# Tower: the inverse norm of the output as one power on POOL and a spreading copy on DVE

## The chip, the cores and the metric

The kernel runs as one program on one core of a Trainium2 chip. The metric is the device time of one execution in microseconds. The five engines work from queues of their own, in order: PE (TensorE), DVE (VectorE), ACT (ScalarE), POOL (GpSimd) and SP (SyncE), which here only issues DMAs.

## The reference, cut to what matters

A small language model: a token tower of two layers, then one layer of linear attention and a gated MLP. All is fp32. The step that the change touches is in the tower's attention:

```python
def _scan_attn(x, ...):                      # x: (32, 256, 128), 8 heads of 16
    ...
    attn = cum_gZ / (cum_g + EPS)
    o = jnp.einsum('bhsd,bhsde->bhse', q, attn)
    nrm = jnp.linalg.norm(o, axis=3, keepdims=True)
    o = o / jnp.maximum(nrm, EPS)            # norm of each head's 16 values
    return o.transpose(0, 2, 1, 3).reshape(Bx, Sx, Dx) @ ok + ob
```

## The kernel before, in words

The 32 sequences are worked off as 16 groups of two. A group is 4 tiles of 128 tokens (J = 4). The tower does each group in two layers (`LAYERS`), and four groups are in flight at once as four streams, each with buffers of its own. When the tower is done, the second part (attention and MLP, names with `b_`) does the 16 groups again with two streams.

The order of the work is a table. `PLACES_A` names every step of a tower group with a layer, a number and a position; `STARTS_A` gives each group's offset; `PLACES_B`, `STARTS_B` and `PREPARE` do the same for the second part and its weights. All steps are sorted by offset plus position, and each engine issues its own steps in that order and waits by semaphores. Only the order inside each engine counts; the positions are not times.

One layer's norm, for one group (so 32 times in all, 16 groups by 2 layers):

- `norm` (ACT) squares the output of `av` into `sq`, 128x512, and copies it to `oT`.
- `sum` (PE, line 889) sums the squares of each head: 32 sums per partition, 4 tiles by 8 heads.
- `chain` (DVE, lines 647 to 665) takes the maximum of the sum and a floor into `m2`, makes `mh` = -0.5 `m2`, a seed `y` by integer arithmetic, and three Newton steps `yy = y*y`, `yy = yy*mh`, `y = (yy + 1.5)*y`. The last of these nine writes the inverse norm spread over each head's 16 values into `sq`, 128x512.
- `unit` (PE, line 897) transposes `sq`, `unit_out` (DVE, line 672) multiplies `oT` by it, `wo` (PE, line 903) is the projection, `wo_out` (DVE, line 678) adds it to `x`.

A layer norm goes over three engines: `stats` (DVE, lines 562, 567, 570) gives mean and variance, `pow` (POOL, line 509) makes the inverse root of a 128x4 tile with an ALU power against a tile of -0.5, `shift` (DVE, line 575) multiplies the mean by it, `xn` (ACT, line 709) normalises, `turn` (PE) transposes, `high` (ACT) and `low` (DVE, line 581) split for the fp32r products `kv`, `q`, `f1`, `head`. POOL also does `bias` (line 514, `x` plus a bias, 128x512), `embed` (line 504) and the indirect DMAs of `gather` (line 479). The gate of the linear attention is `gate_mul` and `gated` on DVE (its last instruction, line 616, writes `gk`), which `state` on PE (line 837) waits for; `state_low` (lines 625 to 629) writes `state`, which `av` on PE (line 870) waits for. `mask` (DVE, line 638) writes the masked scores.

The order on DVE around the first layer's chain of a group g, in the long middle part of the tower: stats of g-1 (its third layer norm), stats of g+1 (first), shift g-1, shift g+1, chain g, low g-1, two `kv_out` of g-1, unit_out g. Around the second layer's: head_out, chain g, mask of g+1, unit_out g.

Of the kernel before, what the change touches and what calls it, by code (L numbers as in the profile page):

```python
# [35 lines left out]
PLACES_A = [("embed", 0, 0, 335), ("stats", 0, 0, 506), ("pow", 0, 0, 630), ("shift", 0, 0, 680), ("xn", 0, 0, 757),  # L36
            ("turn", 0, 0, 592), ("high", 0, 0, 809), ("low", 0, 0, 822), ("bias", 0, 0, 1024), ("q", 0, 0, 941),
            ("q_out", 0, 0, 1183), ("kv", 0, 0, 763), ("kv_out", 0, 0, 881), ("kv", 0, 1, 771),
            ("kv_out", 0, 1, 883), ("conv", 0, 0, 841), ("conv_out", 0, 0, 932), ("conv", 0, 1, 859),
            ("conv_out", 0, 1, 945), ("turn_v", 0, 0, 895), ("vT_out", 0, 0, 1131), ("gate", 0, 0, 992),  # L40
            ("gate_mul", 0, 0, 1284), ("gated", 0, 0, 1354), ("state", 0, 0, 1246), ("state_low", 0, 0, 1467),
            ("qk", 0, 0, 960), ("mask", 0, 0, 961), ("qk", 0, 1, 1198), ("mask", 0, 1, 1450), ("av", 0, 0, 1248),
            ("av", 0, 1, 1311), ("av", 0, 2, 1314), ("av", 0, 3, 1336), ("norm", 0, 0, 1583), ("sum", 0, 0, 1399),
            ("chain", 0, 0, 1684), ("unit", 0, 0, 1481), ("unit_out", 0, 0, 1773), ("wo", 0, 0, 1661),
            ("wo_out", 0, 0, 1842), ("stats", 1, 0, 1853), ("pow", 1, 0, 1993), ("shift", 1, 0, 1903),
            ("xn", 1, 0, 1895), ("turn", 1, 0, 1883), ("high", 1, 0, 2048), ("low", 1, 0, 1945),
            ("bias", 1, 0, 2176), ("f1", 0, 0, 1954), ("gelu", 0, 0, 2248), ("f1", 0, 1, 1956), ("gelu", 0, 1, 2271),
            ("f1", 0, 2, 2017), ("gelu", 0, 2, 2359), ("f1", 0, 3, 2060), ("gelu", 0, 3, 2434), ("f2", 0, 0, 2130),
            ("f2", 0, 1, 2151), ("f2", 0, 2, 2212), ("f2", 0, 3, 2229), ("f2_out", 0, 0, 2474),
            ("stats", 2, 0, 2483), ("pow", 2, 0, 2563), ("shift", 2, 0, 2652), ("xn", 2, 0, 2602),  # L50
            ("turn", 2, 0, 2451), ("high", 2, 0, 2720), ("low", 2, 0, 2701), ("bias", 2, 0, 2993), ("q", 1, 0, 2710),
            ("q_out", 1, 0, 2866), ("kv", 1, 0, 2487), ("kv_out", 1, 0, 2731), ("kv", 1, 1, 2587),
            ("kv_out", 1, 1, 2758), ("conv", 1, 0, 2628), ("conv_out", 1, 0, 2764), ("conv", 1, 1, 2633),
            ("conv_out", 1, 1, 2822), ("turn_v", 1, 0, 2673), ("vT_out", 1, 0, 2830), ("gate", 1, 0, 2823),
            ("gate_mul", 1, 0, 2897), ("gated", 1, 0, 2917), ("state", 1, 0, 2891), ("state_low", 1, 0, 2926),
            ("qk", 1, 0, 2838), ("mask", 1, 0, 2911), ("qk", 1, 1, 2872), ("mask", 1, 1, 2920), ("av", 1, 0, 2892),
            ("av", 1, 1, 2894), ("av", 1, 2, 2919), ("av", 1, 3, 2936), ("norm", 1, 0, 3130), ("sum", 1, 0, 2950),
            ("chain", 1, 0, 2959), ("unit", 1, 0, 3035), ("unit_out", 1, 0, 2984), ("wo", 1, 0, 3076),
            ("wo_out", 1, 0, 3312), ("stats", 3, 0, 3338), ("pow", 3, 0, 3337), ("shift", 3, 0, 3444),
            ("xn", 3, 0, 3526), ("turn", 3, 0, 3283), ("high", 3, 0, 3531), ("low", 3, 0, 3483),  # L60
            ("bias", 3, 0, 3772), ("f1", 1, 0, 3358), ("gelu", 1, 0, 3591), ("f1", 1, 1, 3361), ("gelu", 1, 1, 3680),
            ("f1", 1, 2, 3403), ("gelu", 1, 2, 3709), ("f1", 1, 3, 3441), ("gelu", 1, 3, 3758), ("f2", 1, 0, 3414),
            ("f2", 1, 1, 3468), ("f2", 1, 2, 3480), ("f2", 1, 3, 3626), ("f2_out", 1, 0, 3801),
            ("stats", 4, 0, 3801), ("pow", 4, 0, 3781), ("shift", 4, 0, 3854), ("xn", 4, 0, 3882),
            ("turn", 4, 0, 3882), ("high", 4, 0, 3991), ("low", 4, 0, 3934), ("head", 0, 0, 3942),
            ("head_out", 0, 0, 3957), ("head", 0, 1, 3983), ("head_out", 0, 1, 3994), ("idx", 0, 0, 1577),
            ("gather", 0, 0, 1897), ("gather", 0, 1, 1993), ("gather", 0, 2, 3512), ("gather", 0, 3, 3925),
            ("store", 0, 0, 3837)]
STARTS_A = [434, 1435, 2438, 3441, 4443, 5445, 6445, 7448, 8448, 9448, 10450, 11450, 12454, 13455, 14458, 15457]
PLACES_B = [("b_load", 0, 0, 485), ("b_stats", 0, 0, 411), ("b_pow", 0, 0, 346), ("b_xn", 0, 0, 510),  # L70
            ("b_turn", 0, 0, 1053), ("b_high", 0, 0, 1144), ("b_low", 0, 0, 1023), ("b_turn", 0, 1, 1119),
            ("b_high", 0, 1, 1209), ("b_low", 0, 1, 1075), ("rows_high", 0, 0, 429), ("rows_low", 0, 0, 578),
            ("gram", 0, 0, 658), ("gram_high", 0, 0, 787), ("gram_low", 0, 0, 787), ("gram", 1, 0, 723),
            ("gram_high", 1, 0, 887), ("gram_low", 1, 0, 809), ("t1", 0, 0, 760), ("t1_even", 0, 0, 869),
            ("t1_odd", 0, 0, 812), ("t1", 0, 1, 763), ("t1_even", 0, 1, 919), ("t1_odd", 0, 1, 845),
            ("keys", 0, 0, 826), ("keys_out", 0, 0, 947), ("keys", 0, 1, 834), ("keys_out", 0, 1, 974),
            ("r", 0, 0, 988), ("r_high", 0, 0, 1007), ("r_low", 0, 0, 976), ("r", 0, 1, 1015),
            ("r_high", 0, 1, 1059), ("r_low", 0, 1, 1016), ("m", 0, 0, 1036), ("m", 0, 1, 1041), ("m", 0, 2, 1054),
            ("m_high", 0, 0, 1164), ("m_low", 0, 0, 1034), ("attn", 0, 0, 1144), ("attn_out", 0, 0, 1129),
            ("t1", 1, 0, 844), ("t1_even", 1, 0, 1014), ("t1_odd", 1, 0, 941), ("t1", 1, 1, 1000),  # L80
            ("t1_even", 1, 1, 1038), ("t1_odd", 1, 1, 977), ("keys", 1, 0, 1017), ("keys_out", 1, 0, 1119),
            ("keys", 1, 1, 1023), ("keys_out", 1, 1, 1147), ("r", 1, 0, 1060), ("r_high", 1, 0, 1164),
            ("r_low", 1, 0, 1053), ("r", 1, 1, 1097), ("r_high", 1, 1, 1167), ("r_low", 1, 1, 1071),
            ("m", 1, 0, 1126), ("m", 1, 1, 1131), ("m", 1, 2, 1135), ("m_high", 1, 0, 1223), ("m_low", 1, 0, 1107),
            ("attn", 1, 0, 1165), ("attn_out", 1, 0, 1132), ("b_stats", 1, 0, 1143), ("b_pow", 1, 0, 1156),
            ("b_xn", 1, 0, 1210), ("b_turn", 1, 0, 1211), ("b_high", 1, 0, 1367), ("b_low", 1, 0, 1213),
            ("b_turn", 1, 1, 1222), ("b_high", 1, 1, 1380), ("b_low", 1, 1, 1218), ("b_gate", 0, 0, 1515),
            ("b_up", 0, 0, 1624), ("silu", 0, 0, 1724), ("hid", 0, 0, 1744), ("hid_high", 0, 0, 1812),
            ("hid_low", 0, 0, 1923), ("b_gate", 1, 0, 1576), ("b_up", 1, 0, 1728), ("silu", 1, 0, 1780),
            ("hid", 1, 0, 1769), ("hid_high", 1, 0, 1849), ("hid_low", 1, 0, 2004), ("b_gate", 2, 0, 1583),  # L90
            ("b_up", 2, 0, 1762), ("silu", 2, 0, 1791), ("hid", 2, 0, 1955), ("hid_high", 2, 0, 2438),
            ("hid_low", 2, 0, 2057), ("b_gate", 3, 0, 1634), ("b_up", 3, 0, 1843), ("silu", 3, 0, 2001),
            ("hid", 3, 0, 2018), ("hid_high", 3, 0, 2491), ("hid_low", 3, 0, 2077), ("b_gate", 4, 0, 1767),
            ("b_up", 4, 0, 2432), ("silu", 4, 0, 2072), ("hid", 4, 0, 2436), ("hid_high", 4, 0, 2494),
            ("hid_low", 4, 0, 2435), ("b_gate", 5, 0, 1862), ("b_up", 5, 0, 2436), ("silu", 5, 0, 2076),
            ("hid", 5, 0, 2439), ("hid_high", 5, 0, 2498), ("hid_low", 5, 0, 2449), ("down", 0, 0, 2368),
            ("down", 1, 0, 2406), ("down", 2, 0, 2440), ("down", 3, 0, 2447), ("down", 4, 0, 2492),
            ("down", 5, 0, 2499), ("add", 0, 0, 2485), ("add", 1, 0, 2486), ("send", 0, 0, 2488)]
# [1427 lines left out]
```

## Time and profile before

| what | value |
|---|---|
| median of 3 runs | 2023.23 us (2022.75 to 2024.51) |
| the profiled execution | 2023.51 us |
| its span, first to last instruction | 2021.6 us |
| PE busy | 1854.7 us, 92% |
| DVE busy | 1183.7 us, 59% |
| ACT busy | 723.1 us, 36% |
| POOL busy | 443.7 us, 22% |
| tower | about 55 to 950 us |
| second part | from about 935 us on |

The page's slices show two stages. In the tower, PE stands at 9 tenths or more, DVE at 8 and POOL at 2 to 3. In the second part PE stands at 9, DVE at 4. Between the two is a dip with transfers. DVE work can reach the time only in the tower.

### The profile page before, as it was taken

The numbers are of one execution on the slowest core, as the hardware profiler recorded it, in microseconds if no ns is written. First come the engines' busy times: TensorE is split into PE (matmuls) and PEld (weight loads), VectorE is DVE, ScalarE is ACT, GpSimd is POOL, SyncE is SP. The second block draws the span as 40 slices with busy tenths as digits, with TensorE's granted clock in tenths as the row PEclk, the third lists the DMA queues.
The fourth block names the chain that finished last, engine by engine and source line by source line (L and its number), as shares of the span: only waits on it lengthen the run. The fifth ranks groups of instructions, "written<-read, shape, count | busy, mean of one in ns | idle before, by whom it ended". The sixth has DMA issues, their size and how long they took to land.

```text
span 2021.6 us, 41920 instructions
## 1 busy us (share of the span) xinstructions
PE 1854.7 (92%) x17154; PEld 1586.4 (78%) x17154; DVE 1183.7 (59%) x3021; ACT 723.1 (36%) x1448; POOL 443.7 (22%) x393
## 2 busy tenths in 40 slices
...
GB/s 94 7 4 7 17 17 17 17 18 17 17 16 17 16 14 12 12 32 92 60 2 22 22 22 3 20 22 22 16 7 22 22 22 1 22 22 22 1 22 21
DMA packets 28699, 42.45 MB, mean 21 GB/s; under 512 B 6240, under 2 KB 22112, under 8 KB 28512
## 3 DMA queue, kind: packets, MB, share of 16 engines
...
q0 software_dynamic: 2048, 4.20, 0.8%
...
## 4 chain that ended last, share of the span: by engine, by line
PE 57%; DVE 28%; issue 6%; POOL 3%; DMA 3%; SPq 1%; ACT 1%; DVEq 0%; POOLq 0%; ACTq 0%
PE ps L1314 11%; PE ps L1316 10%; PE ps L1315 10%; DVE att L638 5%; PE ps L1364 3%; PE ps L1380 3%; DMA h<-h_rows 3%; DVE bxn L1179 3%; PE ps L753 2%; DVE stats L562 2%; DVE bstats L1163 2%; PE ps L811 2%; PE ps L903 2%; PE ps L755 2%; PE ps L754 2%
## 5 line engine op out<-in xcount | busy, mean ns | idle before, releaser
L1153 POOL TENSOR_TENSOR hids_low<-hid,hids_high 128x512 fp32r<-128x512 f32 x96 | 137.8, 1442 | 606.1 <-ACT hids_high L1300 606.0
L509 POOL TENSOR_TENSOR rstd<-var,minus_half 128x4 f32<-128x4 f32 x80 | 83.2, 1040 | 607.0 <-DVE var L570 605.9
L709 ACT ACTIVATE xn<-x,shift,rstd 128x128 f32<-128x128 f32 x320 | 131.6, 484 | 163.0 <-DVE shift L575 162.9
L638 DVE TENSOR_TENSOR att<-ps,causal 128x512 f32<-128x512 f32 x256 | 158.3, 678 | 14.5 <-PE ps L856 14.5
L1314 PE MATMUL ps<-r_high,wq_high 128*128 128x256 f32 x512 | 148.9, 291 | 0.7 <-issue 0.7
L1316 PE MATMUL ps<-r_high,wq_low 128*128 128x256 f32 x512 | 144.8, 283 | 0.0
L1315 PE MATMUL ps<-r_low,wq_high 128*128 128x256 f32 x512 | 144.8, 283 | 0.0
L919 PE MATMUL ps<-w_f,wide 128*128 128x128 f32 x1024 | 130.0, 278 | 0.1
L919 PEld LDWEIGHTS ps<-w_f,wide 128*128 128x128 f32 x1024 | 122.2, 193 | 6.4 <-issue 5.0
L1300 ACT ACTIVATE hids_high<-hid 128x512 fp32r<-128x512 f32 x96 | 59.8, 630 | 146.8 <-PE ps L1316 134.6
L1314 PE MATMUL ps<-wd_high,hids_high 128*128 128x256 f32 x384 | 111.3, 290 | 0.7 <-POOL hids_low L1153 0.7
L1294 ACT ACTIVATE silu<-ps 128x512 f32<-128x512 f32 x96 | 55.4, 596 | 155.3 <-DVE hid L1229 86.3
L1315 PE MATMUL ps<-wd_low,hids_high 128*128 128x256 f32 x384 | 108.5, 283 | 0.0
L1316 PE MATMUL ps<-wd_high,hids_low 128*128 128x256 f32 x384 | 108.5, 283 | 0.0
L748 ACT ACTIVATE wide<-ps,b_f 128x512 f32<-128x512 f32 x128 | 84.5, 685 | 59.8 <-PE ps L755 59.8
L1202 DVE COPY t<-ps 128x512 f32<-128x512 f32 x64 | 44.1, 689 | 104.8 <-PE ps L1316 104.8
L1314 PE MATMUL ps<-wv_high,gram_high 128*128 128x512 f32 x256 | 105.0, 410 | 0.2 <-issue 0.2
L1210 DVE TENSOR_TENSOR r_low<-ps,r_high 128x512 fp32r<-128x512 f32 x128 | 80.9, 684 | 38.4 <-ACT r_high L1278 38.4
L1278 ACT ACTIVATE r_high<-ps 128x512 fp32r<-128x512 f32 x128 | 67.8, 599 | 97.1 <-PE ps L1380 97.1
L1315 PE MATMUL ps<-wv_low,gram_high 128*128 128x512 f32 x256 | 100.1, 391 | 0.0
L1316 PE MATMUL ps<-wv_high,gram_low 128*128 128x512 f32 x256 | 99.8, 390 | 0.0
L1185 DVE TENSOR_TENSOR bxT_low<-ps,bxT_high 128x512 fp32r<-128x512 f32 x64 | 42.8, 689 | 97.2 <-ACT bxT_high L1251 97.2
...
## 6 DMA issues: line engine op xcount, KB each, us to landing
...
emb<-in_embed,idx POOLq DMA_INDIRECT x64
...
```

What stands on the lines that cost most here:

```text
L509: pool.tensor_tensor(rstd[s][:], var[s][:], minus_half[:], ALU.pow)\
L638: dve.tensor_tensor(masked[:, :, PAIR * g:PAIR * g + PAIR, :], bank("qk", s, l, j, g, t)[:].rearrange("p (n r t) -> p n r t", n=2, r=PAIR) ...
L709: act.activation(xn[s][:, j, :], x[s][:, j, :], ACT.Identity, bias=shift[s][:, j:j + 1], scale=rstd[s][:, j:j + 1]).then_inc(xn_made[s].se ...
L748: act.activation(gl[s][:, j, :], bank("f1", s, l, j, t)[:], ACT.Gelu_apprx_tanh, bias=b_f1[:, l, j:j + 1]).then_inc(gl_made[s].sem, 1)
L919: ins = pe.matmul(out[:, D * j:D * j + D], gl[s][:, f, P * j:P * j + P], w_f2[l][:, f, :], start=(f == 0 and j == 0), stop=(f == FC - 1), ...
L1153: pool.tensor_tensor(hids[1][:, halves, :], hid[:, half, :], hids[0][:, halves, :].bitcast(F32), ALU.subtract).then_inc(hid_low[s].sem, 1)
L1179: ins = dve.tensor_scalar(xn[s][:, j, :], h[s][:, j, :], mv[s][:, j, 0:1], rstd[s][:, j:j + 1], ALU.subtract, ALU.mult)
L1210: dve.tensor_tensor(low, bank("r", s, b, k, t)[:], high.bitcast(F32), ALU.subtract)\
L1278: act.activation(r[0][:, 2 * k:2 * k + 2, :].rearrange("p k n -> p (k n)"), bank("r", s, b, k, t)[:], ACT.Copy).then_inc(r_high[s].sem, 1)
L1314: pe.matmul(out, lhsT[0], rhs[0], start=start, stop=False, **kw)
L1315: pe.matmul(out, lhsT[0], rhs[1], start=False, stop=False, **kw)
L1316: return pe.matmul(out, lhsT[1], rhs[0], start=False, stop=stop, **kw)
```

## The change

`chain` keeps only the maximum. A new step `root` on POOL raises the 32 values per partition to the power -0.5, and a new step `spread` on DVE copies the result into `sq`, each value over 16 columns. `unit` waits for the third signal in place of the twelfth. The tile of -0.5 grows from 4 to 32 columns and two small tiles go. All tables of the order are new.

```diff
-    minus_half = spare_room.take("minus_half", [P, J])
+    minus_half = spare_room.take("minus_half", [P, J * HEADS])
...
-    NORM = 12
+    NORM = 3
...
-            pool.tensor_tensor(rstd[s][:], var[s][:], minus_half[:], ALU.pow)\
+            pool.tensor_tensor(rstd[s][:], var[s][:], minus_half[:, 0:J], ALU.pow)\
                 .then_inc(ln_rstd[s].sem, 1)
+        elif step == "root":
+            pool.wait_ge(norm_step[s].sem, norm_step[s].at(t, NORM * l + 1))
+            pool.tensor_tensor(y[s][:], m2[s][:], minus_half[:], ALU.pow).then_inc(norm_step[s].sem, 1)
...
             dve.tensor_tensor(m2[s][:], bank("sum", s, l, t)[:, 0:J * HEADS], floor[s][:], ALU.max)\
                 .then_inc(g.sem, 1)
-            dve.wait_ge(g.sem, g.at(t, k + 1))
-            dve.tensor_scalar(mh[s][:], m2[s][:], -0.5, None, ALU.mult).then_inc(g.sem, 1)
-
-            dve.tensor_scalar(y[s][:].bitcast(I32), m2[s][:].bitcast(I32), -0.5, RSQRT_SEED,
-                              ALU.mult, ALU.add).then_inc(g.sem, 1)
-            for n in range(3):
-                dve.wait_ge(g.sem, g.at(t, k + 3 + 3 * n))
-                dve.tensor_tensor(yy[s][:], y[s][:], y[s][:], ALU.mult).then_inc(g.sem, 1)
-                dve.wait_ge(g.sem, g.at(t, k + 4 + 3 * n))
-                dve.tensor_tensor(yy[s][:], yy[s][:], mh[s][:], ALU.mult).then_inc(g.sem, 1)
-                dve.wait_ge(g.sem, g.at(t, k + 5 + 3 * n))
-                if n < 2:
-                    dve.scalar_tensor_tensor(out=y[s][:], in0=yy[s][:], scalar=1.5, in1=y[s][:],
-                                             op0=ALU.add, op1=ALU.mult).then_inc(g.sem, 1)
-                else:
-                    spread = [P, J * HEADS, HD]
-                    dve.scalar_tensor_tensor(out=sq[s][:], in0=yy[s][:].unsqueeze(2).to_broadcast(spread),
-                                             scalar=1.5, in1=y[s][:].unsqueeze(2).to_broadcast(spread),
-                                             op0=ALU.add, op1=ALU.mult).then_inc(g.sem, 1)
+
+        elif step == "spread":
+            dve.wait_ge(norm_step[s].sem, norm_step[s].at(t, NORM * l + 2))
+            dve.tensor_copy(sq[s][:], y[s][:].unsqueeze(2).to_broadcast([P, J * HEADS, HD]))\
+                .then_inc(norm_step[s].sem, 1)
```

The new tables, sorted out for the middle of the tower:

- DVE, first layer of group g: stats g-1, shift g-1, stats g+1, chain g, low g-1, shift g+1, spread g, two `kv_out` of g-1, f2_out, unit_out g.
- DVE, second layer: head_out, chain g, spread g, mask of g+1, unit_out g.
- POOL, first layer: pow g-1, pow g+1, root g, then the `bias` of g and the `bias` of g-2, then pow. Second layer: two `bias`, root g, then the pow of g's next layer norm.
- PE, from `sum` to `unit` of the first layer: before f1, f2, f1, turn, f2, f2; now turn, f2, f2, kv, kv, f2. Of the second: before f1, f1, qk, head, gate, f1; now the same without the last f1.

## Rows read from the trace of the kernel before

**Rows 1.** Busy time per stretch: one tower group, then a stretch of the second part
```profile
485.40:537.50 52.10, 48.87 (x526) 41.24 (x526) 43.86 (x130) 24.81 (x54) 15.94 (x16) 1.00 0.05 17
...
1400.00:1600.00 200.00, 193.46 (x1633) 167.94 (x1633) 88.11 (x172) 57.30 (x108) 35.12 (x27) 1.00 0.05 17
```

**Rows 2.** Waits of PE in the group 537.5 to 589.6: total, times, longest
```profile
PE ps L837 <- DVE gk L616: 1.7, 2, 1.0
PE ps L870 <- DVE state L629: 0.7, 2, 0.4
PE ps L897 <- DVE sq L665: 0.4, 1, 0.4
PE ps L903 <- DVE h_out L672: 0.2, 1, 0.2
```

**Rows 3.** The chain that ended last, 480 to 600: start, length, piece
```profile
536.38 1.02 POOL rstd L509
537.46 1.13 issue
540.91 0.70 DVE sq L665
541.65 0.66 PE ps L897 x4
```

**Rows 4.** Groups by line on DVE: busy, mean ns, idle before
```profile
L647 DVE TENSOR_TENSOR m<-ps,floor 128x32 f32<-128x32 f32 x32 | 6.0, 186 | 15.5 <-PE ps L889 15.5
L650 DVE TENSOR_SCALAR mh<-m 128x32 f32<-128x32 f32 x32 | 5.8, 180 | 1.1
L652 DVE TENSOR_SCALAR y<-m 128x32 int32<-128x32 int32 x32 | 5.6, 174 | 0.0
L656 DVE TENSOR_TENSOR yy<-y 128x32 f32<-128x32 f32 x96 | 18.4, 192 | 3.3
L658 DVE TENSOR_TENSOR yy<-yy,mh 128x32 f32<-128x32 f32 x96 | 21.0, 219 | 3.3
L661 DVE SCALAR_TENSOR_TENSOR y<-yy,y 128x32 f32<-128x32 f32 x64 | 12.3, 192 | 2.2
L665 DVE SCALAR_TENSOR_TENSOR sq<-yy,y 128x512 f32<-128x512 f32 x32 | 22.1, 692 | 1.1
```

**Rows 5.** Timeline of DVE: start, length, instruction; second layer's chain, then first's
```profile
485.33 1.24 DVE L575 SCALAR_TENSOR_TENSOR shift<-mv,rstd 128x4 f32<-128x4 f32 x1 [1.06 <-POOL rstd L509]
...
516.09 0.19 DVE L647 TENSOR_TENSOR m<-ps,floor 128x32 f32<-128x32 f32 x1 [0.80 <-PE ps L889]
...
518.42 0.69 DVE L665 SCALAR_TENSOR_TENSOR sq<-yy,y 128x512 f32<-128x512 f32 x1
...
536.13 0.17 DVE L570 TENSOR_SCALAR var<-mv 128x4 f32<-128x4 f32 x1
...
537.42 1.24 DVE L575 SCALAR_TENSOR_TENSOR shift<-mv,rstd 128x4 f32<-128x4 f32 x1 [1.06 <-POOL rstd L509]
538.59 0.18 DVE L647 TENSOR_TENSOR m<-ps,floor 128x32 f32<-128x32 f32 x1
...
541.52 0.68 DVE L581 TENSOR_TENSOR xT0l<-ps,xT0h 128x512 fp32r<-128x512 f32 x1
```

**Rows 6.** Groups by line on POOL: busy, mean ns, idle before
```profile
L509 POOL TENSOR_TENSOR rstd<-var,minus_half 128x4 f32<-128x4 f32 x80 | 83.2, 1040 | 607.0 <-DVE var L570 605.9
...
L514 POOL TENSOR_TENSOR x<-x,b_o 128x512 f32<-128x512 f32 x32 | 41.1, 1284 | 2.8 <-ACT xn L709 2.0
...
L504 POOL TENSOR_TENSOR x<-emb,pos 128x256 f32<-128x256 f32 x32 | 22.4, 718 | 0.1
```

**Rows 7.** Timeline of POOL beside the first layer's chain
```profile
537.37 1.28 POOL L514 TENSOR_TENSOR x<-x,b_f 128x512 f32<-128x512 f32 x1
```

**Rows 8.** Two lines of DVE by themselves: durations ns min/median/max
```profile
L526 DVE COPY att<-att x5: 220/221/227, 24.0 to 24.6; 128x128 f32<-128x128 f32 x5
...
L575 DVE SCALAR_TENSOR_TENSOR shift<-mv,rstd x80: 148/210/1846, 56.6 to 948.4; 128x4 f32<-128x4 f32 x80
```

**Rows 9.** Waits of DVE in the group 485.4 to 537.5
```profile
DVE shift L575 <- POOL rstd L509: 2.1, 2, 1.1
DVE h_out L689 <- PE ps L755: 1.8, 1, 1.8
...
DVE m L647 <- PE ps L889: 0.8, 1, 0.8
```

More of the change, by code:

```diff
@@ L33 @@
 GK_SLOTS, ATT_SLOTS = 1, 2
[L36 to L98, printed above, removed]
@@ L111 @@
-RSQRT_SEED = float(0x5F3759DF)
+PLACES_A = [("embed", 0, 0, 183), ("stats", 0, 0, 583), ("pow", 0, 0, 744), ("shift", 0, 0, 665), ("xn", 0, 0, 819),
+            ("turn", 0, 0, 581), ("high", 0, 0, 821), ("low", 0, 0, 718), ("bias", 0, 0, 1846), ("q", 0, 0, 927),
+            ("q_out", 0, 0, 1206), ("kv", 0, 0, 668), ("kv_out", 0, 0, 787), ("kv", 0, 1, 693),
+            ("kv_out", 0, 1, 839), ("conv", 0, 0, 767), ("conv_out", 0, 0, 947), ("conv", 0, 1, 785),
+            ("conv_out", 0, 1, 959), ("turn_v", 0, 0, 826), ("vT_out", 0, 0, 1193), ("gate", 0, 0, 1111),
+            ("gate_mul", 0, 0, 1136), ("gated", 0, 0, 1303), ("state", 0, 0, 1290), ("state_low", 0, 0, 1486),
+            ("qk", 0, 0, 965), ("mask", 0, 0, 968), ("qk", 0, 1, 1253), ("mask", 0, 1, 1397), ("av", 0, 0, 1290),
+            ("av", 0, 1, 1301), ("av", 0, 2, 1323), ("av", 0, 3, 1331), ("norm", 0, 0, 1506), ("sum", 0, 0, 1424),
+            ("chain", 0, 0, 1657), ("root", 0, 0, 1763), ("spread", 0, 0, 1684), ("unit", 0, 0, 1579),
+            ("unit_out", 0, 0, 1713), ("wo", 0, 0, 1607), ("wo_out", 0, 0, 1749), ("stats", 1, 0, 1767),
+            ("pow", 1, 0, 2031), ("shift", 1, 0, 1862), ("xn", 1, 0, 1925), ("turn", 1, 0, 1821),
+            ("high", 1, 0, 1986), ("low", 1, 0, 1887), ("bias", 1, 0, 2341), ("f1", 0, 0, 1946),
+            ("gelu", 0, 0, 2229), ("f1", 0, 1, 1952), ("gelu", 0, 1, 2404), ("f1", 0, 2, 2176), ("gelu", 0, 2, 2451),
+            ("f1", 0, 3, 2185), ("gelu", 0, 3, 2459), ("f2", 0, 0, 2253), ("f2", 0, 1, 2263), ("f2", 0, 2, 2268),
+            ("f2", 0, 3, 2269), ("f2_out", 0, 0, 2534), ("stats", 2, 0, 2571), ("pow", 2, 0, 2661),
+            ("shift", 2, 0, 2573), ("xn", 2, 0, 2662), ("turn", 2, 0, 2437), ("high", 2, 0, 2738),
+            ("low", 2, 0, 2666), ("bias", 2, 0, 3352), ("q", 1, 0, 2631), ("q_out", 1, 0, 2882), ("kv", 1, 0, 2570),
+            ("kv_out", 1, 0, 2692), ("kv", 1, 1, 2574), ("kv_out", 1, 1, 2696), ("conv", 1, 0, 2601),
+            ("conv_out", 1, 0, 2852), ("conv", 1, 1, 2603), ("conv_out", 1, 1, 2869), ("turn_v", 1, 0, 2624),
+            ("vT_out", 1, 0, 2874), ("gate", 1, 0, 2683), ("gate_mul", 1, 0, 2820), ("gated", 1, 0, 2874),
+            ("state", 1, 0, 2853), ("state_low", 1, 0, 2882), ("qk", 1, 0, 2739), ("mask", 1, 0, 2873),
+            ("qk", 1, 1, 2812), ("mask", 1, 1, 2881), ("av", 1, 0, 2872), ("av", 1, 1, 2873), ("av", 1, 2, 2910),
+            ("av", 1, 3, 2915), ("norm", 1, 0, 3145), ("sum", 1, 0, 2937), ("chain", 1, 0, 2950),
+            ("root", 1, 0, 3414), ("spread", 1, 0, 2959), ("unit", 1, 0, 3175), ("unit_out", 1, 0, 2985),
+            ("wo", 1, 0, 3228), ("wo_out", 1, 0, 3176), ("stats", 3, 0, 3205), ("pow", 3, 0, 3479),
+            ("shift", 3, 0, 3350), ("xn", 3, 0, 3468), ("turn", 3, 0, 3307), ("high", 3, 0, 3475),
+            ("low", 3, 0, 3569), ("bias", 3, 0, 3851), ("f1", 1, 0, 3349), ("gelu", 1, 0, 3657), ("f1", 1, 1, 3367),
+            ("gelu", 1, 1, 3694), ("f1", 1, 2, 3397), ("gelu", 1, 2, 3701), ("f1", 1, 3, 3413), ("gelu", 1, 3, 3797),
+            ("f2", 1, 0, 3417), ("f2", 1, 1, 3473), ("f2", 1, 2, 3505), ("f2", 1, 3, 3582), ("f2_out", 1, 0, 3708),
+            ("stats", 4, 0, 3742), ("pow", 4, 0, 3955), ("shift", 4, 0, 3824), ("xn", 4, 0, 3911),
+            ("turn", 4, 0, 3881), ("high", 4, 0, 3998), ("low", 4, 0, 3920), ("head", 0, 0, 3930),
+            ("head_out", 0, 0, 3926), ("head", 0, 1, 3994), ("head_out", 0, 1, 3994), ("idx", 0, 0, 1711),
+            ("gather", 0, 0, 1656), ("gather", 0, 1, 2186), ("gather", 0, 2, 3621), ("gather", 0, 3, 3632),
+            ("store", 0, 0, 3944)]
@@ new lines @@
+STARTS_A = [527, 1531, 2530, 3535, 4534, 5537, 6539, 7546, 8546, 9551, 10552, 11551, 12555, 13554, 14554, 15551]
+PLACES_B = [("b_load", 0, 0, 340), ("b_stats", 0, 0, 564), ("b_pow", 0, 0, 522), ("b_xn", 0, 0, 671),
+            ("b_turn", 0, 0, 1012), ("b_high", 0, 0, 1056), ("b_low", 0, 0, 1038), ("b_turn", 0, 1, 1072),
+            ("b_high", 0, 1, 1210), ("b_low", 0, 1, 1130), ("rows_high", 0, 0, 547), ("rows_low", 0, 0, 711),
+            ("gram", 0, 0, 728), ("gram_high", 0, 0, 855), ("gram_low", 0, 0, 742), ("gram", 1, 0, 761),
+            ("gram_high", 1, 0, 937), ("gram_low", 1, 0, 875), ("t1", 0, 0, 776), ("t1_even", 0, 0, 943),
+            ("t1_odd", 0, 0, 838), ("t1", 0, 1, 780), ("t1_even", 0, 1, 965), ("t1_odd", 0, 1, 889),
+            ("keys", 0, 0, 798), ("keys_out", 0, 0, 966), ("keys", 0, 1, 919), ("keys_out", 0, 1, 1010),
+            ("r", 0, 0, 938), ("r_high", 0, 0, 1025), ("r_low", 0, 0, 949), ("r", 0, 1, 941), ("r_high", 0, 1, 1026),
+            ("r_low", 0, 1, 980), ("m", 0, 0, 985), ("m", 0, 1, 1024), ("m", 0, 2, 1025), ("m_high", 0, 0, 1161),
+            ("m_low", 0, 0, 1096), ("attn", 0, 0, 1124), ("attn_out", 0, 0, 1160), ("t1", 1, 0, 959),
+            ("t1_even", 1, 0, 1042), ("t1_odd", 1, 0, 1004), ("t1", 1, 1, 1010), ("t1_even", 1, 1, 1130),
+            ("t1_odd", 1, 1, 1027), ("keys", 1, 0, 1027), ("keys_out", 1, 0, 1181), ("keys", 1, 1, 1039),
+            ("keys_out", 1, 1, 1183), ("r", 1, 0, 1044), ("r_high", 1, 0, 1201), ("r_low", 1, 0, 1106),
+            ("r", 1, 1, 1046), ("r_high", 1, 1, 1208), ("r_low", 1, 1, 1112), ("m", 1, 0, 1084), ("m", 1, 1, 1097),
+            ("m", 1, 2, 1111), ("m_high", 1, 0, 1210), ("m_low", 1, 0, 1142), ("attn", 1, 0, 1163),
+            ("attn_out", 1, 0, 1163), ("b_stats", 1, 0, 1168), ("b_pow", 1, 0, 1074), ("b_xn", 1, 0, 1210),
+            ("b_turn", 1, 0, 1207), ("b_high", 1, 0, 1521), ("b_low", 1, 0, 1212), ("b_turn", 1, 1, 1211),
+            ("b_high", 1, 1, 1674), ("b_low", 1, 1, 1216), ("b_gate", 0, 0, 1479), ("b_up", 0, 0, 1660),
+            ("silu", 0, 0, 1799), ("hid", 0, 0, 1780), ("hid_high", 0, 0, 1900), ("hid_low", 0, 0, 2092),
+            ("b_gate", 1, 0, 1616), ("b_up", 1, 0, 1885), ("silu", 1, 0, 1846), ("hid", 1, 0, 1871),
+            ("hid_high", 1, 0, 2071), ("hid_low", 1, 0, 2200), ("b_gate", 2, 0, 1653), ("b_up", 2, 0, 1907),
+            ("silu", 2, 0, 2021), ("hid", 2, 0, 1974), ("hid_high", 2, 0, 2472), ("hid_low", 2, 0, 2230),
+            ("b_gate", 3, 0, 1799), ("b_up", 3, 0, 1938), ("silu", 3, 0, 2026), ("hid", 3, 0, 2072),
+            ("hid_high", 3, 0, 2480), ("hid_low", 3, 0, 2259), ("b_gate", 4, 0, 1906), ("b_up", 4, 0, 2426),
+            ("silu", 4, 0, 2080), ("hid", 4, 0, 2436), ("hid_high", 4, 0, 2484), ("hid_low", 4, 0, 2409),
+            ("b_gate", 5, 0, 1944), ("b_up", 5, 0, 2433), ("silu", 5, 0, 2181), ("hid", 5, 0, 2441),
+            ("hid_high", 5, 0, 2486), ("hid_low", 5, 0, 2482), ("down", 0, 0, 2320), ("down", 1, 0, 2377),
+            ("down", 2, 0, 2435), ("down", 3, 0, 2442), ("down", 4, 0, 2482), ("down", 5, 0, 2486),
+            ("add", 0, 0, 2482), ("add", 1, 0, 2486), ("send", 0, 0, 2440)]
```

28 lines of the change are left out of this document (13 added, 15 removed).

## The prediction, made before the changed kernel was seen

> **What bounds the kernel now.** First the busy time per stretch [rows 1]. The tower repeats itself every 52.1 us, once per group: the first layer's long `shift` starts at 485.33 and again at 537.42 [rows 5]. In such a period PE is busy 48.9 us and DVE 43.9; in the second part, 200 us hold 193.5 of PE and 88 of DVE. So only the tower can feel DVE, and even there PE has 3.2 us per group to give. Next the waits of PE in one group [rows 2]: 1.7 us for `gk`, 0.7 for `state`, 0.4 for the spread norm, 0.2 for `unit_out`, 3.0 together, all for DVE. This is the most that a faster DVE can return: 3.0 x 16 = 48 us. Last the waits of DVE [rows 9]: 2.1 us for POOL's power (two), some for PE. The chain that ended last [rows 3] runs, before the first layer's norm, through exactly these: power on POOL 1.02, a `shift` that takes 1.13 us longer than its work, the norm chain, the transpose on PE.
>
> **What goes.** Per chain the DVE loses `mh` 0.180, the seed 0.174, three `y*y` of 0.192, three products of 0.219, two closings of 0.192, and the spread closing of 0.692 [rows 4]: 0.180 + 0.174 + 0.576 + 0.657 + 0.384 + 0.692 = 2.66 us. The whole chain, from the maximum's start to the end of the spread, takes 518.42 + 0.69 - 516.09 = 3.0 us [rows 5], and nothing of DVE's lies in between.
>
> **What comes: the copy.** No row has a copy of 128x512 with a spread source inside SBUF. Above it stands the two-input form that it replaces, 0.692 [rows 4]; the copy of 128x128 from a spread source took 0.221 [rows 8]. A two-input form takes 0.192 for 32 columns and 0.692 for 512, so 1.04 ns a column and 0.16 fixed [rows 4]; at that rate 128 columns would take 0.29. The 0.221 fits half the rate (0.16 + 128 x 0.52 ns = 0.227), so I take 0.16 + 512 x 0.52 ns = 0.43 us. Bounds 0.43 and 0.69.
>
> **What comes: the power.** This is the open price, R. The row for the same operation is the 128x4 of `pow`, 1.04 us [rows 6]. POOL's other two-input forms take 0.718 at 256 columns and 1.284 at 512: 2.2 ns a column and 0.15 fixed [rows 6]. So of the power's 1.04 us some 0.88 is neither. If that is paid once per instruction, 28 more columns add 0.06: R = 1.1 us. If it is paid per column (0.22 us each), R = 0.15 + 32 x 0.22 = 7.2 us. The rows don't decide this. I take R = 1.3, near the only row of a power, a little above its lower bound, and keep both ends.
>
> **What comes: the waits.** `root` waits for the maximum, `spread` for `root`, with everything on DVE queued behind `spread` (two `kv_out`, `unit_out`; in the second layer `mask`). Second layer: maximum 0.19, hop 0.1, R, hop 0.1, copy 0.43, so R + 0.8 = 2.1 us in place of 3.0, and POOL has nothing ready behind this root. DVE gains 0.9. First layer: in the order of before, from the end of the second `var` (536.30) DVE waits 1.06 for POOL, then `shift` needs 1.24 instead of 0.15, then 3.0 of chain, then `low`, until 542.2 [rows 5]. `shift` ends at 538.66, and the `bias` that POOL began behind its power ends at 538.65 [rows 7]: a DVE instruction with two SBUF inputs stood still until POOL was through. The longest of 80 `shift` is 1.85 us, the shortest 0.148 [rows 8]. The Trainium skill (SBUF — State Buffer, "SBUF: two separate sides") says why: VectorE and GpSimd share one port pair as an exclusive lock, which a POOL instruction holds for its whole length, against two-input and double-rate DVE instructions. The row agrees. Without the lock the first layer would gain 1.3 us more than I count here. With it the new order costs: `shift` g-1 now waits for its power alone (1.1 us), so stats g+1 and its `var` end 1.3 later, at 537.6; POOL does pow g+1 until 538.8, then `root` until 538.8 + R; `shift` g+1 has two inputs and stands behind `root`; `spread` is of the double-rate kind and stands behind the `bias` that POOL starts next (1.28). DVE is done at 538.8 + 0.2 + 1.28 + 0.45 + R = 540.7 + R, with `low` already behind it. At R = 1.3 that is 542.0 against 542.2: nearly no gain. `unit` on PE would start then instead of at 541.65 [rows 3]; its place in PE's order is about as far behind `sum` as before (two f1 fewer, two kv more).
>
> **The sum.** Per group DVE gains 0.9 + 0.2 = 1.1 us at R = 1.3, and breaks even where 2R costs as much, at R near 1.85. Of the 1.1 I pass on half: the second layer's gain stands ahead of the `gk` and `state` waits of PE (the larger ones, [rows 2]), while the first layer's `unit` comes 0.4 later. 0.5 us x 16 groups = 8 us. The root's load on POOL costs nothing: 2R on top of 15.9 in 52.1 us [rows 1]. The second part has new tables too, with PE at 97% [rows 1]; I cost that at 0, plus or minus 6. So the profiled execution's 2023.5 becomes 2015.5, and against the median (2023.23, 0.3 lower) 2015.2 us.
>
> **The rivals.**
> 1. *The power is paid per column.* R = 7.2. Then the first layer costs 7.2 - 1.5 = 5.7 us more of DVE, the second 7.2 + 0.8 - 3.0 = 5.0, together 10.7 per group. DVE has 52.1 - 43.9 = 8.2 us of idle time there. If all of it absorbs, 2.5 us per group stay, if none, 10.7; the middle is 6.6 x 16 = 106 us, so 2129 us (2063 to 2194). For it: 4 columns already cost 1.04 us, against 0.16 of plain overhead. Against it: nothing in the rows. It decides for slower from R = 1.85 on.
> 2. *In between.* The power has a fixed part and a column part of some 50 ns, R = 2.5. DVE loses 2 x (2.5 - 1.85) = 1.3 per group, half of it reaches PE: 0.65 x 16 = 10 us, 2034 us (2028 to 2050, where all of it does and the tables add their 6). For it: a power worked out in a loop has something of both kinds. Against it: no row shows the split.
> 3. *DVE is shorter and nothing comes of it.* PE is at 94% of a tower group [rows 1], DVE's gain turns into longer waits for PE (`head_out` 1.8, `chain` 0.8, [rows 9]), and the late `unit` of the first layer gives the rest back. 2023 us (2019 to 2027).
>
> That the change does not do what it says can hardly be: ten DVE instructions of every chain are gone from the program.
>
> **How the numbers follow.** Forecast 0.42, with its own range 2004 to 2019; no effect 0.20; in between 0.16; per column 0.22. About 0.2% is what a measurement of this kernel can tell from no change. Faster by more: 0.42. Within: 0.20. Slower: 0.16 + 0.22 = 0.38. The range reaches from 2004 up into the per-column case, to 2095, leaving out some 0.16 above and 0.03 below.
>
> **What would show each step.** The group of the 128x32 power on POOL: 1.1, 2.5 or 7. The copy: 0.43 or 0.69, its longest near 1.7 where the `bias` stands in front. The first layer's `shift` as long as the root. The idle time of DVE before `spread`: about R + 0.1 in the second layer. DVE busy some 50 us less in all, a tower period of 51.6 us and a `gk` wait of PE under 1.7 if I am right; a period of 55 or more and PE waiting for `sq` and for what stands behind `spread` if the power is paid per column. What would make me wrong first is R; next the new tables, which move every step and which I took as neutral.

## The result, and the profile after

The changed kernel takes 2117.4 us (2115.3 to 2120.3) against 2023.0 of the kernel before beside it: a ratio of 1.046, interval 1.0445 to 1.0477. It is slower by 94 us. My forecast was 2015.2, in the range 2004 to 2095; the time lies above both. It is near the first rival (2129, 2063 to 2194), to which I had given 0.22. One execution of a later kernel, the one with ten short POOL instructions, took 5518 us for no reason that a trace shows, and no ratio here contains it.

The page of the kernel after, its head, the chain that ended last and two of the groups by line (busy, mean ns, idle before and who ended it):

```profile
span 2115.1 us, 41632 instructions
...
PE 1879.2 (89%) x17154; PEld 1620.4 (77%) x17154; DVE 1094.9 (52%) x2701; ACT 734.5 (35%) x1448; POOL 614.2 (29%) x425
...
PE 57%; DVE 23%; POOL 12%; issue 4%; DMA 2%; SPq 1%; ACT 1%; DVEq 0%; POOLq 0%; ACTq 0%
...
L511 POOL TENSOR_TENSOR y<-m,minus_half 128x32 f32<-128x32 f32 x32 | 174.1, 5439 | 158.0 <-DVE m L648 158.0
...
L653 DVE COPY sq<-y 128x512 f32<-128x512 f32 x32 | 30.4, 951 | 152.3 <-POOL y L511 152.3
```

DVE is busy 89 us less, 37 of them in `shift`, whose long cases [rows 8] are nearly gone (14.3 us in 80 instead of 51.5), and stands 152 us idle in front of the spreading copy. A part of these stalls only moved: two steps of `gated` with two SBUF inputs took 6.1 us each in 32 before and now take 17.3 and 17.0:

```profile
L608 DVE TENSOR_TENSOR gate<-gate,b_gate 128x32 f32<-128x32 f32 x32 | 17.3, 541 | 1.1
L611 DVE SCALAR_TENSOR_TENSOR gate<-gate 128x32 f32<-128x32 f32 x32 | 17.0, 531 | 1.1
```

The long ones between 400 and 650 us lie beside a `bias` of POOL (one took 1.20 us at 438.54, the `bias` ran from 438.42 to 439.69). POOL, which held 3% of the chain that ended last, holds 12%. The power of 128x32 takes 5.44 us.

The waits of PE and of DVE from 200 to 850 (total, times, longest):

```profile
PE ps L884 <- DVE sq L653: 53.3, 22, 3.7
PE ps L824 <- DVE gk L617: 7.5, 9, 2.0
PE ps L857 <- DVE state L630: 5.9, 17, 0.4
PE ps L890 <- DVE h_out L659: 5.6, 6, 0.9
...
DVE sq L653 <- POOL y L511: 103.2, 22, 5.6
DVE x L665 <- PE ps L890: 31.4, 16, 2.9
```

Against [rows 2], PE no longer waits most for `gk` but for the spread norm, 2.4 us per chain. Every one of the 22 chains in the stretch has it.

One first layer and one second, on POOL and DVE:

```profile
563.60 5.45 POOL L511 TENSOR_TENSOR y<-m,minus_half 128x32 f32<-128x32 f32 x1 [8.85 <-DVE m L648]
...
588.92 5.43 POOL L511 TENSOR_TENSOR y<-m,minus_half 128x32 f32<-128x32 f32 x1 [0.42 <-DVE m L648]
594.31 1.26 POOL L515 TENSOR_TENSOR x<-x,b_f 128x512 f32<-128x512 f32 x1
...
563.33 0.19 DVE L648 TENSOR_TENSOR m<-ps,floor 128x32 f32<-128x32 f32 x1 [0.79 <-PE ps L876]
569.09 0.43 DVE L653 COPY sq<-y 128x512 f32<-128x512 f32 x1 [5.57 <-POOL y L511]
...
588.65 0.19 DVE L648 TENSOR_TENSOR m<-ps,floor 128x32 f32<-128x32 f32 x1 [1.29 <-PE ps L876]
589.84 0.69 DVE L582 TENSOR_TENSOR xT0l<-ps,xT0h 128x512 fp32r<-128x512 f32 x1 [1.00 <-ACT xT0h L701]
590.45 0.15 DVE L576 SCALAR_TENSOR_TENSOR shift<-mv,rstd 128x4 f32<-128x4 f32 x1
594.38 1.47 DVE L653 COPY sq<-y 128x512 f32<-128x512 f32 x1 [3.78 <-POOL y L511]
```

In the second layer DVE does nothing between the maximum and the copy, 5.57 us. In the first it does `low` and `shift`, waits 3.78, and then the copy takes 1.47 us instead of 0.43, because POOL went straight on to the `bias` (594.31 to 595.57). Before, the whole chain took 3.0 us [rows 5].

The span from one group's first-layer maximum to the next is 58.1 us on average of four (415.35 to 647.59) against 52.0 before. So the tower lost 6.1 x 16 = 98 us. From the start of the last `pow` of the tower to the end of the span it is 9 us less than before (2115.1 - 1049.9 = 1065.2 against 2021.6 - 947.3 = 1074.3). The same stretch is 1064.7 to 1069.8 us in every kernel below that has the new tables, and 1075.2 in the one that has the old ones: the second part gained with its new tables. The rest is startup and the tower's end.

PE's granted clock fell too. The busy time from 300 to 800, of before and then of after (PE, PEld, DVE, ACT, POOL, clock):

```profile
300.00:800.00 500.00, 473.48 (x5066) 399.34 (x5067) 420.82 (x1248) 239.68 (x507) 144.99 (x137) 1.00 0.05 16
```

```profile
300.00:800.00 500.00, 442.27 (x4553) 375.52 (x4552) 324.15 (x928) 219.77 (x463) 228.39 (x146) 0.96 0.04 14
```

The timeline of PE after shows one place where it falls:

```profile
569.57 0.66 PE L884 MATMUL ps<-ident,sq 128*128 128x128 f32 x4 [1.91 <-DVE sq L653]
569.98 0.47 PE L740 MATMUL ps<-xT0h,w_f10h 128*128 128x512 f32 x1
570.29 0.43 PE L741 MATMUL ps<-xT0l,w_f10h 128*128 128x512 f32 x1
570.52 0.63 PE L742 MATMUL ps<-xT0h,w_f10l 128*128 128x512 f32 x1
570.95 0.63 PE L740 MATMUL ps<-xT0h,w_f10h 128*128 128x512 f32 x1
571.37 0.63 PE L741 MATMUL ps<-xT0l,w_f10h 128*128 128x512 f32 x1
```

The products start 0.23 us apart, then 0.43: the lower of the clock's two levels, 1.2 GHz, shortly after a wait of 1.91 us.

The same rows split the loss. At 52.1 us per group PE was busy 473.48 / 500 x 52.1 = 49.4 us and idle 2.8; at 58.1 it is busy 51.4 and idle 6.7. So of the 6.0 us per group 3.9 are longer waits, and 2.0 are the same matrix products taking longer.

### The profile page after: what moved, and what is told of

Same layout as the page of the kernel before. It is cut to its first block, busy times and chain, and to the rows that moved or that the text cites. A ratio compares the mean times of both kernels' runs of the same rounds, so it can differ in the third digit from the quotient of the medians.

```text
span 2115.1 us, 41632 instructions
## 1 busy us (share of the span) xinstructions
PE 1879.2 (89%) x17154; PEld 1620.4 (77%) x17154; DVE 1094.9 (52%) x2701; ACT 734.5 (35%) x1448; POOL 614.2 (29%) x425
## 4 chain that ended last, share of the span: by engine, by line
PE 57%; DVE 23%; POOL 12%; issue 4%; DMA 2%; SPq 1%; ACT 1%; DVEq 0%; POOLq 0%; ACTq 0%
PE ps L1301 11%; PE ps L1302 10%; PE ps L1303 10%; POOL y L511 8%; DVE att L639 5%; PE ps L1351 3%; PE ps L1367 3%; DVE bxn L1166 3%; PE ps L798 3%; PE ps L906 2%; DVE bstats L1150 2%; PE ps L865 2%; PE ps L890 2%; PE ps L740 2%; DMA h<-h_rows 2%
## 5 line engine op out<-in xcount | busy, mean ns | idle before, releaser
L511 POOL TENSOR_TENSOR y<-m,minus_half 128x32 f32<-128x32 f32 x32 | 174.1, 5439 | 158.0 <-DVE m L648 158.0
L1130 POOL TENSOR_TENSOR brstd<-bvar,minus_half 128x4 f32<-128x4 f32 x32 | 32.9, 1030 | 265.1 <-DVE bvar L1158 265.1
L653 DVE COPY sq<-y 128x512 f32<-128x512 f32 x32 | 30.4, 951 | 152.3 <-POOL y L511 152.3
L1216 DVE TENSOR_TENSOR hid<-silu,ps 128x512 f32<-128x512 f32 x96 | 64.3, 683 | 78.9 <-PE ps L1303 78.9
```

The lines of the kernel that those rows point to most:

```text
L511: pool.tensor_tensor(y[s][:], m2[s][:], minus_half[:], ALU.pow).then_inc(norm_step[s].sem, 1)
L1216: dve.tensor_tensor(hid[:, uses.place["hid", s, b, t], :], silu[:, uses.place["silu", s, b, t], :], bank("b_up", s, b, t)[:], ALU.mult).th ...
```

## The experiments

Each kernel was timed beside the kernel before on the same chip. The last four kernels (Newton step on DVE, the same with the bias moved, chain behind `low`, first root short) ran on another chip, where the kernel before takes 2026.3 us instead of 2023; between the two groups the ratios are to be compared, not the times. The theory was W: what costs the time is the wait for the power, whose length is R; DVE waits at `spread` and PE at `unit`. The rivals were the new tables (O), the shared port (L), and, once W had stood, how the wait reaches the end.

### The new tables alone, and the old tables with the new norm

```diff
# the new tables; root and spread gone
         elif step == "chain":
             ... max(sum, floor)
+            ... mh, seed and three Newton steps, as before
```

> The changed kernel's tables with the norm chain of before (seed and three Newton steps on DVE, no root, no spread). Theory W (the time is the wait for the 128x32 power, 5.44 us, which DVE sits out behind spread and PE behind unit): the new tables alone cost little, 2017 to 2030 us, tower period about 52 us. Rival O (the new tables lost the time, whatever the norm does): 2080 us or more.

Measured 2053.6 us, ratio 1.0148 (1.0131 to 1.0165). Neither expectation holds: the tables alone cost 30 us with the old norm, more than W allowed, less than O wanted. The waits of PE from 300 to 800 name the place:

```profile
PE ps L754 <- DVE xT0l L582: 9.6, 3, 3.3
PE ps L754 <- DVE xT2l L582: 6.4, 2, 3.3
PE ps L754 <- DVE xT3l L582: 6.4, 2, 3.3
PE ps L754 <- DVE xT1l L582: 6.2, 2, 3.1
```

28.6 us in nine waits for the low half that `low` of g-1 writes. The new tables set the first layer's `chain` in front of that `low`, which is right for one maximum and wrong for 3 us of Newton steps.

```diff
# the old tables
-("chain", 0, 0, 1684), ... ("chain", 1, 0, 2959),
+("chain", 0, 0, 1684), ("root", 0, 0, 1684.1), ("spread", 0, 0, 1684.2), ...
+("chain", 1, 0, 2959), ("root", 1, 0, 3009), ("spread", 1, 0, 2959.2),
```

> The tables of before with the new norm: spread right behind chain on DVE, root on POOL in front of the next bias in the first layer and behind the pow of g+1 in the second. Theory W: as slow as the changed kernel or a little slower, 2110 to 2145 us, since nothing lies between chain and spread in the first layer and the root of the second layer starts later. Rival O: back near 2023 us.

Measured 2163.7 us, ratio 1.069 (1.0671 to 1.0707), 46 us above the changed kernel. O is out: with the old tables the new norm is slower still. It was more than I expected; the granted clock from 300 to 800 is 0.90 there.

### The length of the power

```diff
-            pool.tensor_tensor(y[s][:], m2[s][:], minus_half[:], ALU.pow)
+            pool.tensor_tensor(y[s][:, 0:4], m2[s][:, 0:4], minus_half[:, 0:4], ALU.pow)
```

> The changed kernel with the root over 4 of the 32 columns (the other 28 hold 1.0, so the norm of 28 of 32 heads is left out). The root takes 1.04 us instead of 5.44. Theory W: DVE is freed by what the prediction had for R near 1.1, so 2008 to 2024 us. Rival O: 2080 us or more, since every instruction and its order is still there. Rival L (what costs is that DVE instructions with two SBUF inputs stand behind POOL, not the wait of spread): in between, 2040 to 2070 us, since bias and the spread are as before.

> As the kernel with 4 columns, with 16 of the 32 (the norm of 16 of 32 heads is left out). If the power has a fixed part of 0.41 us and 0.157 us a column, the root takes 2.9 us. Theory W with break-even at R = 1.85 and all of DVE's loss above it on the path: 2 x 1.05 x 16 = 34 us, 2057 us; with half of it, 2040 us. Rival O: 2090 us or more.

With 4 columns 1979.6 us, ratio 0.9789 (0.9773 to 0.9806); with 16 columns 2009.7 us, 0.993 (0.9913 to 0.9946). The power's groups, of 4 columns and then of 16:

```profile
L513 POOL TENSOR_TENSOR y<-m,minus_half 128x4 f32<-128x4 f32 x32 | 32.7, 1020 | 163.2 <-DVE m L650 163.1
```

```profile
L513 POOL TENSOR_TENSOR y<-m,minus_half 128x16 f32<-128x16 f32 x32 | 93.2, 2913 | 161.9 <-DVE m L650 161.8
```

1.02, 2.91 and 5.44 us for 4, 16 and 32 columns lie on one line: 0.39 us and 0.158 us a column. The program differs by nothing but this length, and the three kernels span 138 us. So the length of the power is what costs, as W says; O and L are out as the main cause. But both times lie under what W had expected (2008 to 2024, and 2040 or 2057), by some 30 to 47 us: the size of the gain at a short R was wrong too. With 4 columns the copy is also shorter, 16.9 us in all 32 instead of 30.4, because most copies no longer stand behind a `bias`; that is a part of what the length brings. Per us of R and chain, the first stretch costs (2009.7 - 1979.6) / (1.89 x 32) = 0.50 us, the second (2117.4 - 2009.7) / (2.53 x 32) = 1.33. On a straight line between the last two, the time of before is reached near R = 3.2. In the kernel with 4 columns PE does not wait for the spread norm at all between 300 and 800; it waits for `gk` and `state` alone:

```profile
PE ps L826 <- DVE gk L619: 6.2, 10, 2.0
PE ps L859 <- DVE state L632: 5.6, 17, 0.4
```

### Which layer

```diff
+            c = slice(0, 32 if l else 4)
+            pool.tensor_tensor(y[s][:, c], m2[s][:, c], minus_half[:, c], ALU.pow)
```

> The changed kernel with the power over 4 columns in the first layer (the norm of 28 of 32 heads left out there) and over all 32 in the second. The prediction priced a long root at 5.7 us of DVE per group in the first layer and 5.0 in the second, about alike, which gives the middle of 1979.6 and 2117.4: 2045 to 2052 us. Rival F (only the first layer's root is on the path, as PE waits 3.7 us for its unit; in the second PE has more to do between sum and unit): 2000 us or less. Rival S: the other way round, 2080 us or more.

Measured 2044.0 us, ratio 1.0078 (1.0061 to 1.0094). By the ratios (0.9789, 1.0078, 1.0461) the long root of the second layer costs 2.9%, 58 us, over the kernel with 4 columns, and that of the first layer the other 3.8%, 77 us. F and S are out; the two are of one size, though not quite alike, and the time lies 1 us under the range, by the ratio 6 us. What the first layer's long root costs with a short one in the second was not run.

### The clock

```diff
-            out = claim(pe, "unit", s, l, t, inputs=[(norm_step, NORM * (l + 1))])
+            out = claim(pe, "unit", s, l, t)
+            for n in range(12):
+                pe.matmul(out[:, P * (n % J):P * (n % J) + P], ident[:], w_o[l][:], start=True, stop=True)
+            pe.wait_ge(norm_step[s].sem, norm_step[s].at(t, NORM * (l + 1)))
```

> The changed kernel (2117.4 us) with twelve fp32 products of 128x128 by 128 put on PE in front of every unit, written into the bank that unit overwrites, so that PE works (some 2.7 us) while it waits up to 3.7 us for the spread norm. Theory W plus C (beyond the wait itself, PE's idle stretches bring its granted clock from 1.00 down to 0.96 in the tower, and the slower products are a part of the loss): the granted clock comes back to 0.98 or more and the time falls by 10 to 35 us, to 2082 to 2107 us. Rival W alone: the clock is worth nothing, the time stays at 2117 us or rises by up to the work put in where the wait is shorter than it, 2117 to 2145 us.

Measured 2093.8 us (2117.4 without), ratio 1.0349 (1.0331 to 1.0368). PE does more work and the kernel is 24 us faster. The stretch from 300 to 800:

```profile
300.00:800.00 500.00, 482.21 (x5117) 416.75 (x5116) 338.61 (x978) 224.58 (x471) 230.06 (x150) 1.00 0.05 15
```

PE is busy 482 us instead of 442 and its clock is 1.00 instead of 0.96. DVE waits for the root as before. So of the 108 us between 16 and 32 columns at least 24 are the clock; the work put in costs something itself, so its worth may be more. If it is 24, the other 84 are 1.04 us per us of R and chain. PE's rows give a lower bound: it is idle 2.4 us per group with 16 columns (477.00 of 500 us busy, a period of 51.2) and 6.7 with 32, and 4.3 x 16 = 69 us are 0.86 us per us. Beyond 2.9 us nearly the whole of each further microsecond of the root is on the path.

### The port

```diff
-("bias", 0, 0, 1846) ... ("bias", 3, 0, 3851)
+("bias", 0, 0, 1650) ... ("bias", 3, 0, 3655)
```

> The changed kernel with the two bias steps of POOL that stand right behind the root of the first layer moved ahead of the two pow in front of it. Theory L (the bias holds the port that the spreading copy needs: the copy takes 1.47 us in the first layer and 0.43 in the second): the first layer's copy falls to 0.43, DVE and unit come 1.0 us earlier per group, the time falls by 10 to 20 us, 2097 to 2107 us. Rival: the stall only moves to the shift and the stats in front, or the root itself is held up behind the bias, 2112 to 2135 us.

Measured 2110.1 us, ratio 1.0432 (1.0414 to 1.0451): 7 us faster, less than expected, though the copy did what theory L said (durations ns, min/median/max):

```profile
L653 DVE COPY sq<-y x32: 426/427/429, 92.6 to 1015.2; 128x512 f32<-128x512 f32 x32
```

All 32 copies are short, and PE's wait for the spread norm between 300 and 800 fell from 42.1 to 34.0 us. Its wait for `state` rose from 4.2 to 11.2. The port's price is there (its rival, 2112 to 2135 us, is out), and a good part of it comes back in another wait.

### The spread on ACT

```diff
# and spread moved in the tables: 1684 to 1760, 2959 to 3215
-        dve.tensor_copy(sq[s][:], y[s][:].unsqueeze(2).to_broadcast([P, J * HEADS, HD]))
+        act.activation(sq[s][:], y[s][:].unsqueeze(2).to_broadcast([P, J * HEADS, HD]), ACT.Copy)
```

> The changed kernel with the spreading copy on ACT instead of DVE (first layer: behind high of g-1; second: behind q_out of g+1), so DVE waits for no root. Theory D (the loss comes mostly from DVE's work queued behind spread): 2030 to 2070 us. Theory P (it comes from PE's own wait for unit, which stays 5.4 us and more behind the maximum): 2100 to 2130 us.

Measured 2136.5 us, ratio 1.0562 (1.0543 to 1.0581), above the ranges of both theories. ACT now waits for the root, and behind it stand the `gelu` that PE's `f2` reads. PE's waits from 300 to 800:

```profile
PE ps L906 <- ACT wide L735: 23.4, 7, 3.4
PE ps L884 <- ACT wide L735: 19.5, 7, 2.8
```

This doesn't separate DVE's queue from PE's own wait, as it was meant to. It shows that here moving the waiting instruction only changed whose queue stands still. How much of the loss came through DVE's queue and how much through PE's own wait stays open.

### Other ways to a short root

```diff
# DVE: maximum, mh, seed.  POOL, over 128x32, one Newton step and one of third order:
+  yy = y*y; yy = yy*mh; yy = yy + 1.5; y = y*yy
+  yy = y*y; yy = yy*mh; m2 = 1.5*yy + 2.5; yy = yy*m2; yy = yy + 1.875; y = y*yy
```

> The changed kernel with the root on POOL made of ten short instructions over 128x32 (one Newton step and one of third order, from the seed that DVE makes in two instructions as before) instead of one power. By POOL's rows a two-input form of 32 columns would take some 0.22 us, ten of them with their waits 2.5 to 3.0 us, and DVE gets 0.35 us more. From the kernels with 4 and 16 columns (1979.6 us at R = 1.02, 2009.7 us at R = 2.91) theory W expects 2003 to 2020 us, faster than both kernels. If short POOL instructions cost 0.4 us or more each, R is above 4 and the time 2050 us or more.

Measured 2034.0 us, ratio 1.0055 (1.0033 to 1.0076). The ten instructions start 0.33 us apart, 3.3 us together, and DVE's `mh` and seed add 0.4: R is 3.7 in effect, more than I had expected, and the time misses the range of 2003 to 2020. The line through 16 and 32 columns gives 2043 there; with the wait alone (1.04 instead of 1.33), as the granted clock from 300 to 800 is 1.00 in this kernel, it gives 2036.

```diff
# the Newton step on DVE (three instructions), the third-order step on POOL (six)
```

> The changed kernel's tables; DVE makes maximum, seed and one Newton step (six short instructions), POOL the step of third order in six short instructions (0.33 us each with their waits, as the kernel with ten showed), DVE spreads. From the maximum to the result some 1.1 + 2.0 us, 3.1 us, against 3.7 in the kernel with ten on POOL (2034.0 us) and 2.9 in the one with 16 columns (2009.7 us). Theory W (time follows the span from maximum to result, 42 us for each us above 2.9, 16 below): 2012 to 2022 us, at or a little under the kernel before. Rival: DVE's own time counts as much as the wait, 2030 us or more.

Measured 2009.1 us, ratio 0.9913 (0.9897 to 0.993) against 2026.3 of before on that chip. It is faster than both kernels, by 0.9% and 5%, and 3 us under the range, by the ratio 7 us (2005.4). The rival is out, but the line in R alone put the time too high here. PE's waits for the spread norm are 3.0 us between 300 and 800.

```diff
# the same with the two bias steps moved ahead
```

> The same with the two bias steps moved ahead on POOL, which was worth 7 us with the power. If the gain adds up: 2005 to 2015 us. If short POOL instructions leave the port free often enough for the copy: no difference to the kernel without the move.

Measured 2015.7 us, ratio 0.9949 (0.9932 to 0.9965), 7 us slower than without the move. Neither case of the expectation holds, and with this shorter root the move is a loss. All 32 copies are short again (0.43 us), but PE's wait for `state` between 300 and 800 rose from 5.3 to 14.7 us.

### The old norm in the new tables, once more

```diff
-("chain", 0, 0, 1657)
+("chain", 0, 0, 1673)      # behind low of g-1 and shift of g+1
```

> The new tables with the norm of before (2053.6 us), and the first layer's chain set behind the low of g-1 and the shift of g+1 instead of in front of them. Theory Q (the new tables put the short maximum in front of low, and with 3 us of Newton steps there PE waits 3.3 us per group for the low half that kv reads): that wait goes and the time falls by 20 to 35 us, to 2018 to 2034 us. Rival: the tables lose elsewhere, 2045 us or more.

Measured 2013.3 us, ratio 0.9929 (0.9913 to 0.9946). PE no longer waits for the low half between 300 and 800, as theory Q has it. By the ratios 2.2%, 44 us, come back from moving the chain behind two DVE steps, more than the 20 to 35 expected; the granted clock of the stretch rose from 0.97 to 1.00 as well. And the new tables with the norm of before are 0.7% faster than the kernel before.

## Why the prediction was wrong, point by point

**The price of the power: the step that failed.** I had bounds of 1.1 and 7.2 us and took 1.3, "near the only row of a power". It is 5.44. The row of 128x4 was the nearest in operation, but its size was an eighth, and the bound that I chose assumed that all of its unexplained 0.88 us was fixed. Measured, 0.39 us is fixed and 0.158 a column; of the row's 1.04 us, 0.63 were columns. So the truth lies between the two ends, nearer the column one. With four columns, a fixed 0.88 and a 0.22 per column fit the same row, so the rows could not decide it, and the chance of 0.22 for the column rival was too low for that.

**What a long root costs: near, in part by luck.** The rival had 5.7 us for the first layer and 5.0 for the second at R = 7.2. At R = 5.44 its formulas give 5.44 - 1.5 = 3.9 and 5.44 + 0.8 - 3.0 = 3.2, together 7.2 us of DVE per group, and half to all of it on the path 3.6 to 7.2; the tower lost 6.1 per group. But two errors offset each other: the loss begins at R = 3.2 and not at 1.85, and beyond it each us of root costs 1.33 us and not 0.5 to 1, for the clock comes on top. That each layer carries a large share, 77 and 58 us, was shown by the kernel with a short first root. The sign in DVE's idle time came true: 5.57 us before the second layer's copy, R + 0.1.

**What a short root would bring: mis-sized.** For R near 1.1 the sum would have given some 12 us (1.5 per group, half passed on). The kernel with 4 columns is 43 us faster than before, within the 48 that I had as the most. By the ratios, the new tables account for 0.7% = 14 us of it (old norm, chain behind `low`), of which the second part has 7 to 9 by its own length, and the shorter norm in them for 1.4% = 29 us, 0.9 us per chain. I had passed on half of 1.1 us per group and costed the tables at nothing.

**The break-even: mis-sized.** R = 1.85 was forecast; the runs put it near 3.2. Between 1.0 and 2.9 us the root costs 0.5 of its length only. The likely reason, which no run isolates, is that the tables left DVE `low` and `shift` to do while the root runs, and left PE enough between `sum` and `unit`.

**The copy: right.** 0.43 us was taken, 0.426 to 0.43 measured where nothing stood in front; 1.47 in the first layer behind the `bias` ("near 1.7").

**The `shift` behind the root: wrong.** I had it stand until the root's end, as it stands behind a `bias` in [rows 5, 7]. It took 0.15 us at 590.45, while the root ran from 588.92 to 594.35, and it ran inside the root in 12 first layers, in 0.15 to 0.20 us. So the power does not keep a two-input DVE instruction out over its length. The trace of before had this already. POOL, then DVE:

```profile
525.99 1.04 POOL L509 TENSOR_TENSOR rstd<-var,minus_half 128x4 f32<-128x4 f32 x1 [18.73 <-DVE var L570]
...
526.55 0.19 DVE L607 TENSOR_TENSOR gate<-gate,b_gate 128x32 f32<-128x32 f32 x1
526.78 0.19 DVE L610 SCALAR_TENSOR_TENSOR gate<-gate 128x32 f32<-128x32 f32 x1
```

Two two-input instructions run at their usual 0.19 us inside a power, and they do so in 14 powers of that trace. I read only the additions. Whether a power would hold the double-rate copy is not shown: no copy ran inside one.

**The clock: missing.** The sum had no term for it. It is worth at least 24 us of the 94, by the kernel that fills PE's waits; by the 2.0 us per group that PE's products took longer, it is some 32 (an estimate, since the ends of matrix products are modelled).

**POOL's load at no price: right as far as PE's waits show.** POOL is busy 228 us of 500 instead of 145, and no wait of PE is for it directly. The place of its `bias` has a price of its own, 7 us in the kernel that moved it.

**The account.** From before: new tables -14, shorter norm -29 (to R = 1.02), R to 2.91 +29, R to 5.44 +83 as wait and +24 as clock, together +93. These are differences of neighbouring kernels, so that they add up to the whole is no proof; the kernels with 4, 16 and 32 columns and the one with work in PE's waits carry it, and the border between wait and clock can lie some 14 us further towards the clock.
